# Cross attention of a decoder layer: projections and gate moved to other steps, a pair of maxima put between the two score pairs

## What is computed

```python
x = layernorm(x + self_attention(x))
# cross attention, 8 batches, 512 queries, 1024 keys, 16 heads of 16
q = x @ Wq.T;  k = ctx @ Wk.T;  v = ctx @ Wv.T
attn = softmax(einsum('bnhc,bmhc->bhnm', q, k) * 16**-0.5)
x = layernorm(x + einsum('bhnm,bmhc->bnhc', attn, v).reshape(...) @ Wo.T + bo)
# experts: gate, then softmax over the tokens, then the 8 best tokens of each expert
probs = softmax(x @ gate_w + gate_b, axis=tokens);  vals, idx = top_k(probs, 8)
```

## Time and profile before

| | us |
|---|---|
| median of 3 runs | 1894.79 (1892.1 to 1896.41) |
| the profiled execution | 1894.31 |
| its span, first to last instruction | 1892.4 |
| cross attention, first score to last step | 683.3 to 1679.8 |
| tail of cross attention and experts | 1679.8 to 1892.4 |
| PE busy | 1698.3 (90%) |
| DVE busy | 1232.2 (65%) |
| ACT busy | 848.5 (45%) |
| POOL busy | 595.6 (31%) |
| mean granted TensorE clock | 0.954 |

### The profile page before, as it was taken

How to read it: one execution, slowest core, us unless ns; L and a number is a source line. 1 busy time by engine, 2 the same in 40 slices (tenths; PEclk the granted TensorE clock), 3 DMA queues, 4 the chain that set the end, 5 groups by cost and what they waited for, 6 DMA issues and landing times. The chain is left out here.

```text
span 1892.4 us, 48907 instructions
## 1 busy us (share of the span) xinstructions
PE 1698.3 (90%) x19908; PEld 811.1 (43%) x19908; DVE 1232.2 (65%) x2427; ACT 848.5 (45%) x1029; POOL 595.6 (31%) x955
## 2 busy tenths in 40 slices
PE   5999999999995599999999999999999999976654
PEld 3566666666664233343333333433433334232222
DVE  5767667766753577867778778678677788811004
ACT  3324334334332126655556556566555565651103
POOL 3535555555532715033043140250430410000002
PEclk8999999999997679999999999999999999988887
DMA  7000000000000321111202101111112023245994
GB/s 245 3 3 3 3 3 3 3 3 3 3 3 2 98 73 39 43 44 53 74 1 68 59 26 52 49 51 40 37 53 74 1 76 117 91 178 192 421 419 147
DMA packets 60477, 135.15 MB, mean 71 GB/s; under 512 B 11088, under 2 KB 34128, under 8 KB 52592
## 3 DMA queue, kind: packets, MB, share of 16 engines
q1 hardware_dynamic: 60272, 132.18, 19.3%
HBM read 89.29 MB, written 4.72 MB: 50 GB/s over the span
## 5 line engine op out<-in xcount | busy, mean ns | idle before, releaser
L1583 DVE TENSOR_REDUCE mx<-cpsV 128x1 f32<-128x512 f32 x1024 | 652.7, 685 | 196.4 <-PE cpsV L1284 182.4
L1485 ACT ACTIVATE w<-cpsA 128x1024 f32<-128x1024 f32 x512 | 496.6, 1023 | 291.1 <-PE cpsA L1352 284.5
L1284 PE MATMUL cpsV<-w 96*128 96x512 bf16 x1024 | 329.1, 393 | 34.9 <-DVE mx L1583 23.4
L1352 PE MATMUL cpsA<-w 99*128 99x512 bf16 x1024 | 273.2, 380 | 11.4 <-ACT w L1457 5.9
L1306 PE MATMUL cacc<-w 128*32 128x512 f32 x2048 | 281.1, 604 | 0.4 <-ACT w L1485 0.4
L1139 POOL TENSOR_TENSOR w<-w,zero 128x256 bf16<-128x256 f32 x84 | 48.8, 612 | 579.9 <-ACTq L1458 579.9
L1284 PEld LDWEIGHTS cpsV<-w 96*128 96x128 bf16 x1024 | 85.6, 98 | 304.9 <-DVE mx L1583 203.9
L606 ACT COPY QK<-psA 128x1024 f32<-128x1024 f32 x64 | 64.8, 1013 | 228.2 <-PE psA L363 228.2
L1352 PEld LDWEIGHTS cpsA<-w 99*128 99x128 bf16 x1024 | 92.5, 97 | 148.5 <-ACT w L1457 16.2
L714 POOL TENSOR_TENSOR VP<-V,VPF 128x128 f32<-128x128 f32 (+2 forms) x256 | 128.5, 532 | 41.4 <-PE psA L376 36.1
L363 PE MATMUL psA<-XT,wq 128*128 128x512 f32 x256 | 130.7, 634 | 4.7 <-issue 2.9
(11 more groups left out here) (219 smaller groups left out, 2350.1 us busy)
## 6 DMA issues: line engine op xcount, KB each, us to landing
w<-in_w SPq DMA_DIRECT2D x60, 1024.0 KB, 22.4
w<-w SPq DMA_DIRECT2D x192, 128.0 KB, 2.3
w<-w SPq DMA_DIRECT2D x192, 64.0 KB, 2.0
w<-in_ctxT SPq DMA_DIRECT2D x8, 1024.0 KB, 5.2
XT<-in_xT SPq DMA_DIRECT2D x8, 512.0 KB, 6.1
x_tok<-in_x SPq DMA_DIRECT2D x8, 512.0 KB, 10.1
w<-in_w SPq DMA_DIRECT2D x8, 512.0 KB, 21.3
out_y<-w SPq DMA_DIRECT2D x16, 256.0 KB, 2.4
```

Of the source, the lines that this page charges most:

```text
L1284: nc.tensor.matmul(out, Qst[q // 2][0:ROWS, hh, g * P:(g + 1) * P], Kst[q // 2][0:ROWS, hh, half * BANK:(half + 1) * BANK], start=True, st ...
L1352: last = nc.tensor.matmul(out[:, n * T:(n + 1) * T], Kst[q // 2][0:ROWS + 3, hh, c * P:(c + 1) * P], Qst[q // 2][0:ROWS + 3, hh, :], start ...
L1485: nc.scalar.activation(Pr[:, (2 * s + pp) % 4, :], src, ACT.Exp, scale=CA_SCALE).then_inc(act_evac, 1)
L1583: nc.vector.tensor_reduce(mx[:, q % 2, row, k % 2:k % 2 + 1], full(m[k]), AX_X, ALU.max).then_inc(dve_evac, 1)
```

## The change

Seven constants move. The query projection goes from step 2 to step 4, the merge of the heads from 4 to 2, the output projection from 5 to 4; the gate goes from 13 to 12 (where the second key projection is), its exponentials from 15 to 14, the top-8 probabilities from 16 to 20 (where a value projection is) and their transposition from 17 to 21. Besides, TensorE issues the first two maxima matmuls of a step between the two score pairs, not behind both.

```diff
-OUTPUTS, X1T, PROJECT_V1, PROJECT_Q, MERGE, PROJECT_O, NORM = 1, 0, 1, 2, 4, 5, 7
-PROJECT_K, X2T, COPY_X2, GATE, GATE_EXP, TOP8, TOP8_T, PICK, PICK_T = (7, 12), 9, 10, 13, 15, 16, 17, 28, 29
+OUTPUTS, X1T, PROJECT_V1, PROJECT_Q, MERGE, PROJECT_O, NORM = 1, 0, 1, 4, 2, 4, 7
+PROJECT_K, X2T, COPY_X2, GATE, GATE_EXP, TOP8, TOP8_T, PICK, PICK_T = (7, 12), 9, 10, 12, 14, 20, 21, 28, 29
 PROJECT_V0 = 20
...
                         if c == 0:
                             pe.wait_ge(nm_stacked, (b * QUADS + q + 1) * 16)
-                        for pp in range(2):
+                        def score_pair(pp):
                             out = take_a(("s", s, pp))
                             for n in range(2):
                                 hh = 4 * (q % 2) + 2 * pp + n
...
                             last.then_inc(act_full, 1)
+
+                        score_pair(0)
                     maxima = now and (nxt or s + LEAD < STEPS)
                     if maxima:
                         max_scores(s + LEAD, 0, 1)
+                    if now:
+                        score_pair(1)
```

## The result

The changed kernel takes 1910.76 us in the median (1907.66 to 1913.38) beside 1895.15 for the kernel before: ratio 1.0082, 95% interval 1.0066 to 1.0097. The profiled execution spans 1905.8 us, 13.4 more than before. It is the fastest of the four, with a mean granted clock of 0.952; the other three took 1.8 to 5.7 us longer at 0.946 to 0.950, and no trace says where. So what follows explains 13.4 us, while the medians are 15.6 apart. By the starts of the first scores of each batch, the 13.4 us are: first batch +0.56; middle batches +0.02, +0.39, +0.34, +0.24, +0.33 and +1.34; last batch up to its step 31 +12.31; tail of the cross attention (from there to the first matmuls on expert weights, L1844, before L1840) -2.66; the rest +0.56.

What follows compares the result with a forecast made beforehand. PE was taken as the bound, with only its idle time to win. From the profiled 1894.3 us: +1.7 middle batches, +1.5 first, +2.3 last, +8.4 stall, +1.9 clock, giving 1910.1; range 1893 to 1918.

Steps and rivals of the forecast that it cites:

- M1's wait in a plain step: Plain steps: the second maxima matmul waits for a tile, starting at 0.73 us; 0.09 a step, 1.6 us a batch.
- Rival 2: The second maxima matmul's wait is hidden between the score pairs, so the kernel is faster, 1884 us; chance 0.12.
- The rest of the swap: Maxima between score pairs, beyond plain steps: 2.1 us a batch lost after transpositions and outputs, 0.9 gained at copies.
- Steps 3 to 6: Middle batches: 0.7 us gained in step 6, 1.0 in step 4; 0.65 lost waiting for the output projection's second result.
- Step 8: Middle batches: NORM waits for GpSimd's inverse root, starts some 3.7 us late and delays maxima reductions; 1.45 us lost.
- Steps 12 to 17 and 21: Middle batches: gate under key projection gains 1.07 us in step 14, 0.3 in 13; moved top 8 gains 1.6.
- First batch: +1.5 us: plain steps 0.09 each, 1.6 after transpositions, 1.0 behind outputs, less 1.1 at copies and 2.0 in step 4.
- Last batch: +2.3 us, no projections covering VectorE; 8.4 stall, maxima DMA behind 4 MB of weights; 1.9 for lower clock afterwards.
- Rival 1: Last batch: the maxima DMA does not wait behind the weights, 1900 us; chance 0.12.
- 3: The moves win more: neither NORM's 1.45 us nor the second result's 0.65 is lost; 1897 us, chance 0.10.
- 4: The maxima DMA is late in the middle batches too, by about 1 us; 1916 us, chance 0.12.
- 5: Middle batches: top 8 at step 20 delays `nmT` or stacking, several us a batch from step 28; 1925 us, chance 0.06.

Runs made afterwards that it cites:

- e5: Changed kernel with only the first maxima matmul between the score pairs, and the last batch's maxima DMA issued before the weights: 1886.98 us, ratio 0.9955.
- e4: Moved steps with the old order of scores and maxima, and the last batch's maxima DMA issued before the 4 MB of weights: 1890.41 us, ratio 0.998.
- e1: Changed kernel with all step constants put back, so only the two maxima matmuls between the score pairs remain: 1909.01 us, ratio 1.0068.
- e2: Changed kernel with the moved constants kept and the maxima matmuls behind both score pairs again: 1900.51 us, ratio 1.0028.
- e11: Kernel before with only query projection, merge and output projection moved, DMAs in the old order: 1904.78 us, ratio 1.0052.
- e9: Kernel before with only gate, exponentials and top 8 moved, and the maxima DMA issued ahead of stacking and weights: 1878.79 us, ratio 0.9913.
- e3: Changed kernel with the last batch's maxima DMA issued before the 4 MB of weights: 1901.48 us, ratio 1.0033.
- e10: Kernel before with gate, exponentials and top 8 moved, maxima DMA issued first, and the first maxima matmul between the score pairs: 1871.41 us, ratio 0.9874.
- e6: As e5, with the first key projection and NORM moved from step 7 to step 8: 1871.90 us, ratio 0.9875.
- e8: As e4, with the first key projection and NORM moved from step 7 to step 8: 1876.80 us, ratio 0.9912.

## Why the prediction was right, and where its steps were off

The forecast was 1910.1 and the median is 1910.76. The mechanisms were there, but the closeness is partly luck. Both halves of the middle batches were sized too high, and cancelled. Besides, the sum was 15.8 above the profiled execution of the kernel before, and the profiled executions differ by 13.4; the median of the changed kernel lies 3.1 above its profiled execution, for which the sum had no term.

- **M1's wait in a plain step** (0.09, forecast M1 at 0.73): right, 2.83 to 2.93, M1 at 0.73. Rival 2 falls by its own criterion, and e5 shows that M1 alone carries the wait.
- **The rest of the swap** (2.1 lost, 0.9 gained): oversized. Comparing the changed kernel with e4 by steps, the losses are 0.20, 0.30, 0.21 and 0.28 in steps 5, 29, 13 and 21 and 0.32 in 18 and 26, together 1.6; the gains are 0.31, 0.31, 0.25 and 0.32 in steps 2, 3, 8 and 10, together 1.2. With the plain steps (some 16 of 0.09) the swap costs 1.9 to 2.1 a batch, not 2.8 to 2.9. The terms that failed are the 0.62 of step 5 and the 0.44 of step 29. The expectation of e1, 1.4 a batch, was then too low.
- **Steps 3 to 6** (0.7 and 1.0 gained, 0.65 lost): step 6 right (0.71 in e4). Step 4 is the term that failed: its gain of 1.0 and loss of 0.65 were to leave 0.35 gained in steps 2 to 5, and e4 has these steps 0.51 longer, 21.91 in place of 21.40. The wait for the second result is 0.92, since the chain takes 1.33 there and not 0.96. Further, step 5 without its output projection takes 3.26, some 0.4 above a plain step: a wait after the transposition of the maxima, which the projection had covered and the sum left out. The two make 0.7 of the 0.86 between forecast and measurement.
- **Step 8** (1.45 lost): right in kind, M1 waits behind a late NORM. In the moves alone it is 1.28 (4.60 less 3.32), in the changed kernel 1.03, and M0 now fills S1's wait. The prediction's 12.8 us from copy to inverse root should be 12.6 by its own terms; NORM waited 3.80, forecast 3.7. What was missed is that NORM's lateness grows as the steps before it shorten, and that this idle time can bring the clock down. In the middle batches of the changed kernel's profiled execution it didn't; in those of e2, e4, e5 and e11 it did.
- **Steps 12 to 17 and 21** (1.4 and 1.6 gained): 1.07 and 1.71 in e9. The 0.3 of step 13 was not there: it stays at 3.25.
- **First batch** (+1.5; its own terms sum to +1.3): +0.56. The moves gave 2.1, forecast 2.0; the swap cost less, as in the middle.
- **Last batch** (+2.3, stall 8.4, clock 1.9): +3.96 in e3, of which 1.57 is a half-clock stretch in step 13, so 2.4. The stall is 7.3, the clock behind it 2.6, together 9.9 in place of 10.3. Rival 1 falls. The stall was sized 1.1 too high for two reasons. The weights took about 12 us and not 13.1: in the kernel before the DMA share is 0.02 already from 1655.6 to 1656.6, so step 24 could start 17.1 us after step 20, forecast 17.7. And steps 20 to 23 take 9.8 without the stand, forecast 9.3. That the tail would give back 2.66 was not in the sum: before, the clock was 0.50 in the stretch from 1684.3 to 1687.7, and with the stand it is 1.00 until 1708. As e1, e9 and e10, without the stand, have -2.64, -2.58 and -2.57, the stand is not its cause; what moves the stretches of low clock in the tail stays open.
- **Rivals 3 to 5**: 3 falls, since both waits came. 4 holds in one batch of six, for 0.54 us, and the margin is thin: with shorter steps (e2, e4, e5, e6, e8) batches 1, 3 and 6 wait 0.2 to 1.1. 5 falls: steps 28 and later are as before but for the swap's share.

So the sum by measured terms is +0.3 a middle batch (2.7 in all, with batch 6, whose step 17 had been 0.75 shorter before than in the other batches and whose step 23 waits 0.54 now), +0.6 in the first, +12.3 in the last, -2.7 in the tail, and +0.6 outside.

Open: whether the load of instructions is what holds a stacking DMA for 1.3 to 2.0 us, where the 0.44 in the chain of step 4 comes from, and which idle times bring the clock down (1.32 us in step 8 of the changed kernel's profiled execution did not).

## What to carry to other kernels

Move short VectorE work under a long projection that is already there; that paid 2.8 us a batch. Moving the projections themselves cost 1.1 a batch as it was done, and even with NORM moved along, what the middle batches won was lost at the end. When a shared pool of PSUM tiles is handed out in turn, count for each job which earlier job must have been read: one matmul between the score pairs was free, the second cost 0.09 in every plain step. Before a job that signals is moved, list what its waiter issues next: here 4 MB of weights got ahead of a 12 KB transfer, and one swapped pair of lines was worth 0.5%.

## What was not expected of the hardware

Idle time of some 1.1 to 1.4 us of PE in the midst of dense work was enough, in some executions of the same step, for the granted clock to fall from 1.00 to 0.50 for 3.4 us, at about 1.5 us each; with the idle time covered (e6 to e8) no middle batch of a profiled execution showed it. It was not bound to step 8: in e11 the clock fell in step 17 of batch 1 too, from 885.2 to 888.6, and the step took 7.23 in place of 5.64, though the kernel before has the same step with the same idle time and no fall. An idle microsecond on the bound engine can so cost more than a microsecond.
